# Metaformer block on one core: router chain rewritten, convolution entered before all queries are made, band products inside the norm

## The chip, the cores and the metric

One core of one Trainium2 chip runs the whole kernel. The metric is device microseconds (us) of one execution, median of the runs. Engines are called by the profile's names: PE is the matrix engine (PEld its weight loads), DVE the vector engine, ACT the scalar engine, POOL the GpSimd engine, SP the engine whose queue issues most DMA transfers (a DMA moves data between HBM and SBUF, or inside SBUF). SBUF is the working memory with 128 partitions, PSUM the eight banks that PE writes. Each engine works through its own instructions in order and waits on semaphores.

## The reference, cut to what matters

```python
# x: (8, 128, 16, 16), that is 2048 tokens (8 images x 256 places) of 128 channels
n   = layernorm(x)                          # over channels, here in chunks of 512 tokens
qkv = conv1x1(n, w_qkv)                     # 384 channels: queries, keys, values of 8 heads
agg = conv1x1_grouped(conv5x5_depthwise(qkv, w_dw), w_pw)
for h in (qkv heads, agg heads):            # linear attention, relu on q and k
    out = q @ (k^T [v, 1]),  divided by its last column
x = x + batchnorm(conv1x1(out, w_proj))
# mixture of experts 0: 8 experts, width 512, gelu, best 2 of 8 by t @ gate_w.T
# then softmax attention over the 256 places of an image (adds to x)
# mixture of experts 1: 16 experts, width 256, silu(gate) * up, best 2 of 16
```

Both mixtures see tokens normalised over channels; the kernel normalises them with a centred product and a per-token scale.

## The kernel before, in words

**Opening.** `layer_norm` on PE makes, for each of four chunks c of 512 columns, the centred chunk (L1131), then 4 products for the variance (L1138), then the product that spreads the inverse root over the partitions (`ln_spread`, L1148). DVE (`ln_scale`) makes the diagonal for it (L787) and multiplies (L794), giving `xn`. `turn_weights` transposes the weights of queries, keys and values and the small convolution weights inside the norm (L1161 to L1166). `keep_clock` (L1120) are products whose result nobody uses. `head(n, c)` (L1175) is the 1x1 convolution of chunk c; n counts keys, values, queries. ACT evicts each (L579; for queries also through a relu into `q_relu`, L578).

**Bands.** Eight band products (L1187) and one spread (L1192) lay the depthwise and pointwise weights out over the partitions; ACT evicts all nine (L586, L590, semaphore `band_out`). From `dw_band` and `pw_in`, POOL and DVE multiply the weights of the convolution, `cw` (`build_weights`, L321): for each of 12 units four groups, two by POOL and two by DVE, three units ahead of PE at most. A unit is 32 channel groups of keys, values or queries: units 0 to 3 are keys, 4 to 7 values, 8 to 11 queries.

**Convolution.** 48 steps s, four a unit, each ten PE instructions (L1281) on `cmap`, the maps that SP fetches from `heads_raw` unit by unit (L391). PE enters the loop only when all 12 head evictions, the late weight transposes (L1201) and the router product (L1257) are done. `STEPS` says at which s the stages of the first linear attention (L1212 turn, L1224, L1237, L1249) come between: for image n at s = 3n + 1. The second attention, on the convolution's output, comes from s = 38 on.

**Router r (0 and 1).** `token_norm` on PE makes, for 16 tiles of 128 tokens, the centred rows and the logits (L1315) in six banks. ACT evicts the logits (L667), squares the rows (L655), takes roots (L660). DVE then runs a chain in which each `step` waits for the one ahead: the best expert, a mask, the second best (L918 to L924), `chosen` (L926, written with its axes turned), and after PE's counts (`slots`: L1326 to L1338) the slot of each token (L936 to L946), the one-hot tables `block_hot`, `block_val`, `place_hot` (L951 to L956), with which PE inverts the table (L1345). DVE reads the result as `token` and `dest` (L976 to L978). The inverse root `tok_inv` (L900) is made in two halves, one ahead of the slots, one between the two `place_hot`. ACT scales the rows with it (L683, `token_rows`), SP stores them (L363), and POOL gathers the rows of each block by `token` (L518) for the experts (L1379 transposes them, L1369 and L1390 are the two expert products).

POOL also makes tables once, in the opening: `place_id` (128 x 4096), `passed`, and others (L487).

Of the kernel before, what the change touches and what calls it, by code (L numbers as in the profile page):

```python
# [32 lines left out]
F16 = mybir.dt.float16  # L33
# [27 lines left out]
STEPS = {3 * n + 1: (0, n) for n in range(B + 3)} | {4 * 2 * UPT + 6 + n: (1, n) for n in range(B + 1)}  # L61
# [37 lines left out]
def metaformer(nc, x, w_qkv, w_dw, w_pw, w_proj, bn_gamma, bn_beta, bn_mean, bn_var,  # L99
# [10 lines left out]
    with ctx:  # L110
# [15 lines left out]
        place_id = sb("place_id", [128, 128, 2 * TT], F16)  # L126
        pair_id = sb("pair_id", [128, 2, TT], F16)
# [36 lines left out]
        hots = sb("hots", [128, 2, TT, E1])  # L164
# [7 lines left out]
        slot_f = sb("slot_f", [128, 2, TT])  # L172
        slot_i = sb("slot_i", [128, 3, 2, TT], I32)
# [82 lines left out]
        band_mm, band_out = sem("band_mm"), sem("band_out")  # L256
# [180 lines left out]
        def _(pool):  # L437
# [51 lines left out]
            table(place_id[:, :, :], [[1, 128], [0, 2 * TT]], 0, 0)  # L489
# [4 lines left out]
            table(passed[:, :, :], [[128, NI1], [-128, E1 - 1]], 0, 0)  # L494
# [3 lines left out]
            pool.affine_select(out=passed[:, :, :], in_=passed[:, :, :], compare_op=ALU.is_ge, fill=1e6,  # L498
                               base=NB - 1, pattern=[[-1, NI1], [1, E1 - 1]], channel_multiplier=0).then_inc(tables, 1)
# [3 lines left out]
            pool.wait_ge(band_out, 9)  # L503
            for u in range(len(UNITS)):
                for i in (0, 2):
                    build_weights(pool, u, i)

            def moe_pool(r, E):
# [5 lines left out]
                pool.wait_ge(rt_table, 4 * r + 3)  # L514
# [7 lines left out]
                pool.wait_ge(rt_table, 4 * r + 4)  # L522
# [12 lines left out]
        def _(act):  # L535
# [33 lines left out]
            def heads(n, t):  # L569

                for c in range(NCH):
                    act.wait_ge(qkv_mm, NCH * n + c + 1)
                    src = bank[c][:, :].rearrange("p (b y x) -> p b y x", b=2, y=HW)

                    def to(m):
                        return m[:, :, :, 2 * c:2 * c + 2].rearrange("p x y b -> p b y x")
                    if t == 0:
                        act.activation(to(q_relu), src, ACT.Relu).then_inc(q_relued, 1)  # L578
                    act.activation(to(heads_raw[t]), src, ACT.Copy).then_inc(head_a, 1)  # L579

            heads(0, ORDER[0])

            for k in range(9):
                act.wait_ge(band_mm, k + 1)
                if k < 8:
                    act.activation(dw_band[:, :, :, 2 * k:2 * k + 2].rearrange("p k g x -> p x (k g)"),  # L586
                                   bank[4 + k % 4][:, 0:2 * KS * NG].rearrange("p (x n) -> p x n", x=2),
                                   ACT.Copy).then_inc(band_out, 1)
                else:
                    act.activation(pw_in[:, :, :].rearrange("p o g -> p (o g)"), bank[4][:, 0:G8 * NG],  # L590
                                   ACT.Copy).then_inc(band_out, 1)
            for n in (1, 2):
                heads(n, ORDER[n])

            act.wait_ge(w_ready, 6)
            act.activation(bn[:, 0:1], vec("var"), ACT.Sqrt, bias=eps[:, 2:3]).then_inc(bn_step, 1)
# [21 lines left out]
            for s in range(GU * len(UNITS)):  # L618
                if s in STEPS:
# [28 lines left out]
            def token_scales(r):  # L648
# [14 lines left out]
                for g, tiles in enumerate(ROW_GROUPS):  # L663
                    act.wait_ge(rows_mm, 6 * r + g + 1)
                    a, n = tiles[0], len(tiles)
                    src = bank[ROW_BANKS[r][g]][:, 0:n * (C + E)].rearrange("p (t q) -> p t q", t=n)
                    act.activation(tok_lg[:, a:a + n, 0:E], src[:, :, C:C + E], ACT.Copy).then_inc(tok_logits, 1)  # L667
                    if g < 4:
                        squares(tiles)
                    if g == 3:  # L670
                        roots(0)
                squares(range(12, TT))
# [6 lines left out]
            def token_rows(r):  # L679
                for i in range(TT):  # L680
                    if i % 8 == 0:
                        act.wait_ge(tok_scale, 2 * r + i // 8 + 1)
# [3 lines left out]
            def moe_act(r, E, NI):  # L686
                m = moe[r]
                if r == 0:
                    act.wait_ge(moe_w[0], 48)
                    act.wait_ge(rt_table, 1)  # L690
# [80 lines left out]
        def _(dve):  # L771
# [26 lines left out]
            def conv_weights():  # L798
# [4 lines left out]
                dve.wait_ge(dw_zero, 1)  # L803
                dve.tensor_copy(dw_t[0:G8 * KS, :, :].rearrange("p k g -> p (k g)"), bank[1][0:G8 * KS, 0:KS * NG])\
                    .then_inc(w_ready, 1)
                dve.tensor_copy(pw_t[:, :, :].rearrange("p o g -> p (o g)"), bank[2][0:G8, 0:G8 * NG])\
                    .then_inc(w_ready, 1)

            ln_scale(0, conv_weights)
            dve.wait_ge(w_turned, 2)  # L810
            dve.tensor_copy(wT[:, W_P0:W_P0 + 4, :], bank[6][:, :].rearrange("p (j q) -> p j q", q=128))\
                .then_inc(w_ready, 1)
# [692 lines left out]
```

## Time and profile before

| | us |
|---|---|
| median of 3 runs (lowest, highest) | 446.61 (446.04, 447.75) |
| the profiled execution | 449.81 |
| its span, first to last instruction | 448.1 |
| PE busy, share of the span | 374.2 (84%) |
| DVE, ACT, POOL busy | 238.8, 191.2, 192.3 |
| PE's share of the chain that ended last | 66% |
| mean granted clock of PE | 0.895 |

PE busy is the time with a matmul in flight; the chain is the sequence of work, followed back from the last instruction, in which each piece released the next. Only what lies on it sets the time. The granted clock is a share of 2.4 GHz; its two levels are 1.00 (2.4 GHz) and 0.50 (1.2 GHz), and a stretch between them contains a change.

### The profile page before, as it was taken

How to read it: one execution, taken by the hardware profiler on the slowest of the kernel's cores; microseconds unless marked ns; L12 is line 12 of the kernel's file. 1: busy time of each engine (PE TensorE's matmuls, PEld its weight loads, DVE VectorE, ACT ScalarE, POOL GpSimd, SP SyncE). 2: the span in 40 equal slices, each digit the busy share in tenths (PEclk: the TensorE clock that was granted, in tenths of full speed). 3: DMA queues.
4: the chain of work that ended last, by engine and by line, in shares of the span. 5: the costliest groups of instructions: out<-in, count | busy, mean ns of one | idle time of the engine just before them, and what ended most of it. 6: DMA issues, size and time to landing. Idle time of an engine off the chain costs nothing.

```text
span 448.1 us, 7846 instructions
## 1 busy us (share of the span) xinstructions
PE 374.2 (84%) x2499; PEld 318.3 (71%) x2499; DVE 238.8 (53%) x589; ACT 191.2 (43%) x512; POOL 192.3 (43%) x206
## 2 busy tenths in 40 slices
PE   6998799999989837999999569989636999999903
PEld 3673799999969524999999536665423998888802
DVE  2611355455126382566777457476584466567515
ACT  3089223322322644677666256385443233222213
POOL 9916055356000306777775500000306777566620
PEclk9599699999998965899999969999956799999965
DMA  5013045455238522895111160000012112111146
GB/s 153 0 24 78 17 67 85 62 88 78 28 47 278 145 69 61 266 309 150 55 55 41 38 189 0 1 0 0 1 57 69 54 52 54 42 42 43 42 118 187
DMA packets 44015, 35.27 MB, mean 79 GB/s; under 512 B 3800, under 2 KB 39752, under 8 KB 43976
## 3 DMA queue, kind: packets, MB, share of 16 engines
q1 hardware_dynamic: 36412, 24.70, 21.6%
q0 software_dynamic: 4096, 8.40, 6.4%
q10 hardware_dynamic: 3468, 1.67, 2.6%
q8 instruction: 22, 0.36, 0.4%
q14 instruction: 17, 0.14, 0.1%
HBM read 21.12 MB, written 7.34 MB: 64 GB/s over the span
## 4 chain that ended last, share of the span: by engine, by line
PE 66%; DVE 9%; ACT 7%; DMA 7%; issue 4%; POOL 3%; SPq 1%; ACTq 1%; DVEq 1%; POOLq 0%
PE bank L1369 16%; PE bank L1281 11%; PE bank L1390 10%; PE bank L1237 3%; POOL x_rows L518 3%; PE bank L1131 2%; DMA x_rows<-tok,token 2%; PE bank L1148 2%; DMA ln_sq<-y 2%; ACT heads L579 2%; PE bank L1138 2%; PE bank L1416 2%; PE bank L1457 2%; PE bank L1224 2%; PE bank L1120 2%
## 5 line engine op out<-in xcount | busy, mean ns | idle before, releaser
L1369 PE MATMUL bank<-x_cols,w_block 128*128 x688 | 99.6, 291 | 7.9 <-DVE w_block L1019 5.0
L1369 PEld LDWEIGHTS bank<-x_cols,w_block 128*128 128x128 f32 x688 | 88.7, 202 | 13.5 <-issue 12.3
L518 POOL DMA_INDIRECT x_rows<-tok,token x64 | 61.7, 964 | 52.5 <-DMA tok<-ln_sq 33.6
L525 POOL DMA_INDIRECT y<-wide,dest x64 | 63.2, 987 | 34.2 <-DVE wide L1054 25.6
L1390 PE MATMUL bank<-w_down,h_cols 128*128 x500 | 71.7, 281 | 1.7 <-DVE wide L1054 1.7
L1390 PEld LDWEIGHTS bank<-w_down,h_cols 128*128 128x128 f32 x500 | 64.2, 196 | 2.2 <-issue 2.0
L1281 PE MATMUL bank<-cmap,cw 128*128 128x112 f32 (+2 forms) x480 | 59.0, 281 | 0.3 <-DVE tok_w L854 0.3
L321 POOL TENSOR_TENSOR cw<-pw_in,dw_band 128x640 f32<-128x640 f32 x24 | 37.2, 1571 | 49.6 <-PE bank L1281 38.6
L1281 PEld LDWEIGHTS bank<-cmap,cw 128*128 128x128 f32 x480 | 57.5, 198 | 0.5 <-DVE tok_w L854 0.5
L512 POOL MEMSET wide<- 128x4096 f32 x2 | 7.0, 3511 | 100.5 <-DVE xs L1105 60.6
L1034 DVE TENSOR_TENSOR h_cols<-h_in,bank 128x256 f32<-128x256 f32 x47 | 19.7, 419 | 30.2 <-PE bank L1390 15.1
L1026 DVE TENSOR_TENSOR h_in<-bank,wT 128x512 f32<-128x512 f32 x39 | 27.0, 691 | 16.4 <-PE bank L1369 13.9
L710 ACT ACTIVATE h_cols<-h_in 128x512 f32<-128x512 f32 x39 | 24.6, 630 | 24.1 <-PE bank L1390 19.9
L702 ACT ACTIVATE x_cols<-bank 128x128 f32<-128x128 f32 x64 | 15.4, 270 | 37.9 <-PE bank L1379 37.9
L716 ACT ACTIVATE h_in<-bank 128x256 f32<-128x256 f32 x47 | 18.0, 383 | 30.9 <-PE bank L1369 30.9
L321 DVE TENSOR_TENSOR cw<-pw_in,dw_band 128x640 f32<-128x640 f32 x24 | 23.0, 991 | 5.7 <-PE bank L1281 5.7
L1120 PE MATMUL bank<-ones,ident 128*128 128x512 f32 x24 | 18.2, 893 | 7.3 <-DMA ln_sq<-y 7.3
L699 ACT ACTIVATE w_block<-w_up 128x512 f32 x39 | 23.9, 614 | 0.2 <-PE bank L1369 0.2
L824 DVE TENSOR_TENSOR kvm<-bank,blk 128x128 f32<-128x128 f32 x16 | 4.7, 291 | 34.9 <-PE bank L1224 34.9
L1019 DVE COPY w_block<-w_up 128x512 f32 x47 | 20.9, 447 | 3.1 <-issue 2.4
L725 ACT ACTIVATE wide<-wide,pair_w 128x128 f32<-128x128 f32 x32 | 10.2, 389 | 24.5 <-DMA ln_sq<-y 24.5
L1379 PE MATMUL bank<-ident,x_rows 128*128 128x128 f32 x64 | 15.8, 298 | 4.2 <-DMA x_rows<-tok,token 4.2
(209 smaller groups left out, 602.3 us busy)
## 6 DMA issues: line engine op xcount, KB each, us to landing
cmap<-heads SPq DMA_DIRECT2D x48, 64.0 KB
w_up<-in_L_ffn_w_dram SPq DMA_DIRECT2D x1, 2048.0 KB, 8.7
tok<-ln_sq SPq DMA_DIRECT2D x8, 256.0 KB, 2.3
w_up<-in_L_ffn_gate_w_dram SPq DMA_DIRECT2D x4, 512.0 KB
w_up<-in_L_ffn_up_w_dram SPq DMA_DIRECT2D x4, 512.0 KB
w_down<-in_L_ffn_down_w_dram SPq DMA_DIRECT2D x4, 512.0 KB
wide<-y SPq DMA_DIRECT2D x8, 256.0 KB, 4.5
ln_sq<-y SPq DMA_DIRECT2D x8, 256.0 KB, 5.0
```

The lines of the kernel that those rows point to most:

```text
L321: engine.tensor_tensor(cw[:, u % CWR, i, :, :].rearrange("p k (o x) -> p k o x", x=HW), pw_in[:, :, g].unsqueeze(1).unsqueeze(3).broadcast ...
L518: pool.indirect_dma_start(out=x_rows[:, j % RING, :], out_offset=None, in_=tok_dram[r], in_offset=bass.IndirectOffsetOnAxis(ap=token[r][:, ...
L525: pool.indirect_dma_start(out=y_dram[r], in_=y_acc[:, s * C:(s + 1) * C], in_offset=None, out_offset=bass.IndirectOffsetOnAxis(ap=dest[r][ ...
L699: act.activation(w_block[:, n % 3, :], w_up0[:, bass.ds(e * F0, F0)], ACT.Copy).then_inc(m.w, 1)
L710: act.activation(h_cols[:, j % 2, :], h_in[:, j % 2, :], ACT.Gelu_apprx_tanh)\
L1019: dve.tensor_copy(w_block[:, j % 3, :], w_up[:, bass.ds(e[j] * UP, UP)]).then_inc(m.w, 1)
L1026: dve.tensor_tensor(h_in[:, j % 2, :].rearrange("p (k s) -> p k s", k=M0), bank[2 + j % 2][:, :].rearrange("p (k s) -> p k s", k=M0), wT[: ...
L1034: dve.tensor_tensor(h_cols[:, j % 2, 0:F1], h_in[:, j % 2, 0:F1], bank[2 + j % 2][:, F1:2 * F1], ALU.mult).then_inc(m.h_in, 1)
L1120: pe.matmul(bank[b][:, :], ident[:, :], ones[:, :].unsqueeze(1).broadcast_to([128, 4, 128]), start=True, stop=True)
L1281: mm = pe.matmul(bank[b][:, i * 128 + y0 * B:i * 128 + y1 * B], cw[:, u % CWR, i, k, :], cmap[:, t, v * GU + i, (y0 + k - EDGE) * B:(y1 + ...
L1369: mm = pe.matmul(bank[2 + j % 2][:, i * 128:(i + 1) * 128], w_block[:, j % 3, i * 128:(i + 1) * 128], x_cols[:, bass.ds(at[j], 128)], star ...
L1390: mm = pe.matmul(bank[6 + j % 2][:, 0:C], h_cols[:, j % 2, i * 128:(i + 1) * 128], w_down[:, bass.ds(ej * (K * C) + i * C, C)], start=(i = ...
```

## The change

In the opening, all four variance groups now come first on PE, then `turn_weights`; the unused product of `keep_clock` is gone; spreads, band products and the heads of keys are woven together. ACT evicts bands 0 to 3 and the spread, DVE bands 4 to 7; ACT instead of DVE evicts `dw_t` and `pw_t`. `q_relu` is made by one DVE instruction from `heads_raw`. PE enters the convolution after 10 of the 12 heads; the last two come at s = 2 and 3, the late transposes at s = 6, the router product at s = 10. The first attention starts at s = 12, one image every two and a half steps. POOL makes `place_id`, a new table `block_id`, and `passed` between the `cw` builds. In the router, DVE evicts the logits, `chosen` is written in the order of memory, the slots take four steps, `tok_inv` is one instruction directly behind `chosen`, and `token` and `dest` come ahead of the item tables; POOL waits for `token` alone.

```diff
-STEPS = {3 * n + 1: (0, n) for n in range(B + 3)} | ...
+STEPS = {12 + 5 * n // 2: (0, n) for n in range(B + 3)} | ...
+        BAND_BANKS = (3, 4, 5, 4, 6, 7, 5, 4)
+        PW_BANK = 6
+        HEAD_BANKS = ((0, 1, 2, 3), (7, 5, 4, 6), (2, 3, 7, 5))
 # PE, opening
-            layer_norm(0, lambda c: (x_in[c], 16), between=turn_weights, after=lambda c: head(0, c))
-            (eight band products, the spread, heads 1 and 2, late transposes)
+            for c in range(NCH):
+                pe.wait_ge(x_in[c], 16)
+                pe.matmul(bank[c][:, :], center[:, :], chunk(xs, c), start=True, stop=True).then_inc(ln_cent, 1)
+            (four variance groups)
+            turn_weights()
+            spread_scale(0)
+            spread_scale(1)
+            band_product(0)
+            head(0, 0)
+            spread_scale(2)
+            band_product(1)
+            head(0, 1)
+            spread_scale(3)
+            band_product(2)
+            head(0, 2)
+            band_product(3)
+            head(0, 3)
+            for k in range(4, 8):
+                band_product(k)
+            (the spread of pw_t)
+            for c in range(NCH):
+                head(1, c)
+            head(2, 0)
+            head(2, 1)
 # PE, in the loop of 48 steps
+                if s in (2, 3):
+                    head(2, s)
+                if s == 6:
+                    turn_late()
+                if s == 10:
+                    (router product)
+                if s == 12:
+                    pe.wait_ge(q_relued, 1)
+                    pe.wait_ge(router_out, 1)
 # ACT
+            for k in range(4):
+                act.wait_ge(band_mm, k + 1)
+                act.activation(dw_band[...], bank[BAND_BANKS[k]][...], ACT.Copy).then_inc(band_act, 1)
+                head_copy(0, k)
 # DVE, in the loop of 48 steps
+                if s == 4:
+                    dve.wait_ge(head_a, 3 * NCH)
+                    dve.tensor_scalar(q_relu[...], heads_raw[0][...], 0.0, None, ALU.max).then_inc(q_relued, 1)
+                if s == 7:
+                    late_weights()
 # POOL
             for u in range(len(UNITS)):
                 for i in (0, 2):
                     build_weights(pool, u, i)
+                if u == CWR - 1:
+                    table(place_id[:, :, :], [[1, 128], [0, 2 * TT]], 0, 0)
+                if u == CWR:
+                    table(block_id[:, :, :], [[128, NB], [0, 2 * TT]], 0, 0)
+                if u == CWR + 1:
+                    table(passed[:, :, :], [[128, NI1], [-128, E1 - 1]], 0, 0)
 # DVE, router
-        hots = sb("hots", [128, 2, TT, E1])
+        hots = sb("hots", [128, 2, E1, TT])
+                dve.tensor_tensor(chosen[:, 0:E, :], hots[:, 0, 0:E, :], hots[:, 1, 0:E, :], ALU.add).then_inc(rt_mask, 1)
+                token_inverse(r)
+                step(dve.tensor_tensor(both, both, slot.unsqueeze(1).broadcast_to([128, 2, E, TT]), ALU.mult))
+                step(dve.tensor_reduce(slot_i[...], both.rearrange("p k e t -> p k t e"), AX.X, ALU.max))
+                step(dve.tensor_tensor(slot_parts[...], slot_i[...], low_high[:, :, :], ALU.bitwise_and))
+                step(dve.tensor_copy(place[...], slot_parts[:, :, :]))
 # PE, end of slots
-                keep_clock(1, 2)
+                pe.wait_ge(rows_copied, TT * (r + 1))
+                keep_clock(4, 2)
```

## Rows read from the trace of the kernel before

**Rows 1.** The chain of waits, opening: start us, us, what, count.
```profile
10.00 2.67 PE bank L1138 x24
...
14.56 2.00 PE bank L1120 x2
16.57 1.71 PE bank L1148 x2
18.27 1.50 PE bank L1138 x8
...
23.91 0.86 PE bank L1175 x2
...
27.53 6.48 PE bank L1187 x32
...
46.08 0.91 ACT heads L579
...
48.00 2.47 PE bank L1281 x10
```

**Rows 2.** Busy time by stretch: stretch, length, busy PE, PEld, DVE, ACT, POOL, clock, DMA.
```profile
18.00:22.00 4.00, 4.00 (x12) 2.72 (x11) 2.98 (x7) 0.26 (x1) 4.00 (x6) 0.50 0.00 0
22.00:24.00 2.00, 2.00 (x5) 0.89 (x4) 1.24 (x4) 0.91 (x1) 1.85 (x4) 0.85 0.01 4
...
52.00:54.00 2.00, 2.00 (x14) 2.00 (x14) 0.00 (x0) 0.02 (x1) 0.00 (x0) 0.67 0.00 0
```

**Rows 3.** Timeline of PE: start us, us, engine, line, operation, count, [idle before].
```profile
41.75 0.82 PE L1201 MATMUL bank<-ident,wraw 128*128 128x128 f32 x6
...
101.60 7.97 PE L1281 MATMUL bank<-cmap,cw 128*128 128x128 f32 x70
110.35 0.46 PE L1212 MATMUL bank<-ident,wide 128*128 128x128 f32 x2 [0.79 <-DMA heads<-conv_out]
```

**Rows 4.** Timeline of SP's queue while the first maps are fetched.
```profile
28.67 16.46 SPq L391 DMA_DIRECT2D cmap<-heads  x20
```

**Rows 5.** Timeline of POOL: the largest table, and builds of `cw`.
```profile
15.93 4.18 POOL L487 IOTA place_id<- 128x4096 f16 x1
...
35.53 7.81 POOL L321 TENSOR_TENSOR cw<-pw_in,dw_band 128x640 f32<-128x640 f32 x6 [11.03 <-ACT pw_in L590]
...
107.42 3.86 POOL L321 TENSOR_TENSOR cw<-pw_in,dw_band 128x640 f32<-128x640 f32 x2 [0.62 <-PE bank L1281]
```

**Rows 6.** Timeline around router 0.
```profile
150.19 3.87 PE L1315 MATMUL bank<-tok_w,xs 128*128 128x136 f32 x32
...
154.97 0.29 DVE L918 TENSOR_REDUCE rv<-tok_lg 128x16 f32<-128x128 f32 x1 [3.83 <-ACT tok_lg L667]
...
158.53 0.69 DVE L926 TENSOR_TENSOR chosen<-hots 128x128 f16<-128x128 f32 x1
...
160.36 0.17 DVE L936 COPY ends<-bank 128x8 f32<-128x8 f32 x1 [0.28 <-PE bank L1338]
...
162.41 0.69 DVE L951 TENSOR_TENSOR block_hot<-place_id,place 128x1024 f16<-128x1024 f16 x1
...
167.80 0.18 DVE L977 TENSOR_SCALAR token<-place_of 128x32 int32<-128x32 int32 x1
...
169.92 1.14 POOL L518 DMA_INDIRECT x_rows<-tok,token  x1 [15.21 <-DMA tok<-ln_sq]
```

**Rows 7.** Timeline around router 1.
```profile
320.43 0.42 DVE L918 TENSOR_REDUCE rv<-tok_lg 128x16 f32<-128x256 f32 x1 [3.98 <-ACT tok_lg L667]
...
325.45 1.23 DVE L926 TENSOR_TENSOR chosen<-hots 128x256 f16<-128x256 f32 x1
...
333.60 2.45 PE L1345 MATMUL bank<-block_val,place_hot 128*128 128x32 f16 x32 [5.33 <-DVE place_hot L956]
...
336.92 0.17 DVE L976 CAST place_of<-bank 128x32 int32<-128x32 f32 x1
...
338.38 1.23 POOL L518 DMA_INDIRECT x_rows<-tok,token  x1 [18.36 <-DMA tok<-ln_sq]
```

More of the change, by code:

```diff
@@ L488, in table @@
                           allow_small_or_imprecise_dtypes=True).then_inc(tables, 1)
-            table(place_id[:, :, :], [[1, 128], [0, 2 * TT]], 0, 0)
+            table(low_high[:, 0, :], [[0, 2 * TT]], 127, 0)
+            table(low_high[:, 1, :], [[0, 2 * TT]], (NB - 1) * 128, 0)
             table(pair_id[:, 0, :], [[128, TT]], 0, 1)
@@ L581, in _ @@
[L581 to L596, printed above, removed]
+            act.wait_ge(w_turned, 1)
+            act.wait_ge(dw_zero, 1)
+            act.activation(dw_t[0:G8 * KS, :, :].rearrange("p k g -> p (k g)"), bank[1][0:G8 * KS, 0:KS * NG], ACT.Copy)\
+                .then_inc(dw_ready, 1)
+            act.activation(pw_t[:, :, :].rearrange("p o g -> p (o g)"), bank[2][0:G8, 0:G8 * NG], ACT.Copy)\
+                .then_inc(dw_ready, 1)
@@ L598, in kv_copy @@
+            act.wait_ge(band_mm, 9)
+            act.activation(pw_in[:, :, :].rearrange("p o g -> p (o g)"), bank[PW_BANK][:, 0:G8 * NG],
+                           ACT.Copy).then_inc(band_act, 1)
+            for n in (1, 2):
+                for c in range(NCH):
+                    head_copy(n, c)
             def kv_copy(h, b):
@@ L917, in router @@
-                for src, top, oh in ((lg, m1, oh1), (l2, m2, oh2)):
-                    step(dve.tensor_reduce(top, src, AX.X, ALU.max))
-                    step(dve.tensor_tensor(eq, src, per_e(top), ALU.is_equal))
-                    step(dve.tensor_tensor(sc, eq, rk, ALU.mult))
+                    dve.wait_ge(tables, 15 + E1)
+                step(dve.tensor_reduce(m1, lg, AX.X, ALU.max))
+                step(dve.tensor_tensor(eq, lg, per_e(m1), ALU.subtract))
+                for oh in (oh1, oh2):
+                    if oh is oh2:
+                        step(dve.scalar_tensor_tensor(out=l2, in0=oh1, scalar=MASKED, in1=eq,
+                                                      op0=ALU.mult, op1=ALU.add))
+                        step(dve.tensor_reduce(d, l2, AX.X, ALU.max))
+                        step(dve.tensor_tensor(l2, l2, per_e(d), ALU.subtract))
+                    step(dve.scalar_tensor_tensor(out=sc, in0=(eq if oh is oh1 else l2), scalar=0.0, in1=rk,
+                                                  op0=ALU.is_ge, op1=ALU.mult))
@@ L921, in router @@
                     step(dve.tensor_reduce(mx, sc, AX.X, ALU.max))
                     step(dve.tensor_tensor(oh, sc, per_e(mx), ALU.is_equal))
-                    if oh is oh1:
-                        step(dve.scalar_tensor_tensor(out=l2, in0=oh1, scalar=MASKED, in1=lg,
-                                                      op0=ALU.mult, op1=ALU.add))
-                dve.tensor_tensor(chosen[:, 0:E, :].rearrange("p e t -> p t e"), oh1, oh2, ALU.add).then_inc(rt_mask, 1)
-                step(dve.tensor_tensor(d, m2, m1, ALU.subtract))
+                dve.tensor_tensor(chosen[:, 0:E, :], hots[:, 0, 0:E, :], hots[:, 1, 0:E, :], ALU.add).then_inc(rt_mask, 1)
@@ new lines, in _ @@
+            turn_weights()
[11 more added lines that the diff above has]
+            head(0, 3)
+            for k in range(4, 8):
+                band_product(k)
+            pe.wait_ge(band_dve, 1)
+            pe.wait_ge(dw_ready, 2)
+            pe.matmul(bank[PW_BANK][:, 0:G8 * NG], spread[:, :, :].rearrange("p i x -> p (i x)"),
+                      pw_t[:, :, :].rearrange("p o g -> p (o g)"), start=True, stop=True).then_inc(band_mm, 1)
```

208 lines of the change are left out of this document (113 added, 95 removed).

## Prediction

> **What bounds the kernel now.** I read the page first: the chain that ended last is mostly PE, so I asked of each stage whether PE, or something that PE waits for, ends last. The chain of waits over the opening gives the answer for that part [rows 1]: PE carries it to the band products, and then it changes to ACT, whose evictions of the heads follow each other at 0.91 us until 46.99. PE has nothing to do in that time; the convolution starts only at 48.00. The busy time by stretch shows what the pause costs besides [rows 2]: the clock is 0.50 when the convolution starts and reaches 1.00 only at 53.3 (a mean of 0.67 over 52 to 54 is 0.68 us at the full level). The same view shows 0.50 from the norm to 22.6. In the convolution itself the timeline of PE shows ten instructions in 1.11 us (7.97 over 7 steps plus a little overhead) without gaps, but for one of 0.79 [rows 3]: that stage is PE's alone. The timelines of the two routers show the reverse [rows 6, 7]: PE waits, DVE's chain of small steps sets the time, and at its end POOL's first gather waits not for the token table (ready at 167.98) but for the stored rows, until 169.92.
>
> **The opening, after.** I take PE's order and add the durations. The variances of three chunks end at 12.67 as before. The fourth, 1.50 at the lower level, to 14.2; the transposes take 1.9 (12.67 to 14.56 before), to 16.1; two spreads at 1.71, to 19.5 [rows 1]. DVE has both diagonals by 14.7, ahead of PE. What follows on PE up to the convolution, at the full level: eight band products at 0.81 (6.48 / 8), ten heads and two spreads at 0.86, the last spread of weights some 0.86: 6.5 + 10.3 + 0.9 = 17.7, so 37.2. At the lower level PE takes double. Before, dense work from 14.56 had the clock up at 22.6, with sparse variances (1.50, one column each) in between [rows 1, 2]. After, dense work starts at 16.1 and is not interrupted, so I put the rise between 19.5 and 22.6: 0 to 1.5 us lost, 0.7 taken. Start of the convolution: 37.9 instead of 48.00, 10.1 earlier.
>
> What could be late instead: ACT alternates a band (0.81) and a head (0.91) while PE needs 2.5 for such a pair and a spread, so it keeps up; it has the last band and `pw_in` by 33.5. DVE evicts bands 4 to 7, which the trace has only on ACT. From 480 columns in order to twice that, 0.65 to 1.2 each, four of them end by 32.7 or 34.3; `cw` is then begun at 33.5 to 34.4 and the first group is there at 36.4 at the latest. The maps: the fourth key eviction is at 29.8 instead of 28.6, four issues at 0.82 [rows 4] end at 33.1, plus some 2 to land: 35.1. All are ahead of 37.9, by 1.5 at the least. Only head products, then, stand between; the words "while values and queries are still made" are true of two heads on PE and of eight evictions on ACT.
>
> **The convolution, after.** PE's work in it grows by two heads (1.7), the late transposes (0.82 and one more, 1.0) [rows 3] and the router product (0.3): 3.0. It no longer begins at 0.50: 5.3 us at half speed cost 2.65 [rows 2]. The gap of 0.79 goes, because it waits for aggregated values sent just ahead of s = 38, and the steps of the first attention now lie in front (s up to 37) and give the transfers 3.8 us more. Net: 10.1 - 3.0 + 2.65 + 0.8 = 10.5 us.
>
> Moved past other queues: POOL's builds now have the tables between them. Six builds took 7.81 alone, and two took 3.86 beside DVE's [rows 5], so from 33.5 six end at 41.3 to 45.1, `place_id` (4.18) at 45.5 to 49.3, and unit 3 is built at 48.1 to 53.2. PE wants it at 37.9 + 12 x 1.11 + 3.0 = 54.2. The next tables are smaller and each unit then takes twice as long on PE, so it is covered by 1 to 6 us. Behind DVE's relu at s = 4, which waits for the twelfth eviction (about 44), are builds for unit 3 (wanted at 54) and the late weights (wanted at s = 10, some 51.6): covered by 2 us or more. SP has for a unit 3.3 of maps and 1.4 of sends against 4.45 on PE, but starts four units ahead.
>
> The Trainium skill (SBUF — State Buffer, "Who interferes with whom") says that a DVE instruction with two SBUF inputs, or in a two-port mode, and a GpSimd instruction take a shared port for the whole instruction, so that one of them blocks. The rows agree as far as they go, 1.30 for a POOL build alone and 1.93 beside DVE. By the rule the relu (an estimate of 1.3 us) could wait for all of `place_id`; by the rows 4.18 at most, which still leaves the wanted time of the late weights about met.
>
> **Router 0.** Logits: the last rows are made at 154.06; DVE evicts them itself (0.2) as the groups come and starts its first step near 154.5 instead of 154.97: 0.5. The number of steps to the masks is 11 before and 11 after: 0. `chosen` in order of memory: 0.69 becomes 0.29, the length of the steps of that size: 0.4. From the counts to `block_hot` 2.05 us are spent (160.36 to 162.41); after, a product and a reduction of 256 columns (0.42 each, as in router 1), a mask and a cast (0.2 each) with 0.03 between: 1.34, so 0.7. No reciprocal between the two `place_hot`: 0.1. End: the rows are scaled right after `chosen` (158.6), 16 at 0.27 and 2.3 for the last store, so at 165.3, and the gather waits for `token` instead (about 166.3): 169.92 - 167.98 = 1.95 more. Sum 3.65 [rows 6].
>
> Against it: both masks are now written with a stride. Below, nothing. Above, as `chosen` was: (1.23 - 0.42) / 256 = 3.2 ns more an element [rows 7], 0.8 us here and 1.6 in router 1. The nearest row for 4-byte elements is ACT's strided eviction of a head, 0.91 / 512 = 1.8 ns against 1.0 ns on DVE ((0.42 - 0.29) / 128): 0.8 more, so 0.2 and 0.4; I take those. And PE's two unused products (some 3.4 at the lower level) now end at about 169.3, where the first gathered rows land, and ACT's table loads end near the same time: 0.35 lost. Router 0: 3.1 us.
>
> **Router 1.** The same with 256 columns: logits 0.6, `chosen` 1.23 to 0.42 0.8, slots 0.7, reciprocal 0.1. PE's inversion ends at 336.05 but DVE reads it at 336.92, behind the item tables; that order is turned: 0.9. `token` is ready at 337.3 and the gather starts at 338.38, waiting for stored rows: 1.1. Less 0.4 for the stride, and 0.1 for PE's unused products: 3.7 us [rows 7].
>
> **Sum.** 10.5 + 3.1 + 3.7 = 17.3. Of the profiled execution, 449.81, that leaves 432.5 (span 430.8); the median of the runs is 3.2 lower than that execution, so I forecast 446.6 - 17.3 = 429.3.
>
> **Rivals.** (a) As summed, 425.5 to 432: 0.62. Its low end is the strides at nothing (0.6), the clock up at once (0.7), and a shorter low stretch at the start of the experts, where PE begins closer behind its unused products (2); its high end the other bounds.
> (b) Strides cost what `chosen` did: 0.6 more in router 0, 1.2 more in router 1, and 1 for the evictions of bands if those then pass the heads: 432. For it, only the 2-byte row; against it, ACT's. Chance 0.12. The Trainium skill (SBUF — State Buffer, "Door 1: The DMA port swizzle") says that each access which crosses into a new 16-byte line pays a penalty, which would make this stride dear; the rows show it for ACT's and for `chosen`.
> (c) The builds set the pace: POOL at 1.93 a build and blocked by DVE besides; if every table costs as much as `place_id`, units 3 to 5 each come 1.5 to 2 late and 5 us of the 10.5 go: 434.3. For it, two builds of 3.86; against it, the slack above. Chance 0.12.
> (d) Gathers don't start earlier, because the stored rows still land last: 3.05 of the routers goes, 432.4. Against it, 165.3 against 166.3. Chance 0.07.
> (e) Slower: the clock isn't granted with bands, heads and waits for evictions alternating. At 0.50 to the end of the heads and 5.3 us into the convolution, PE gets to it at 19.5 + 35.4 = 54.9, 6.9 later; with the 3.0 added, 0.8 saved, and 6.8 from the routers that is 2.3 us slower, 448.9. It decides only if the low stretch goes on past about 50; before, the clock came up under the same products with longer pauses. Chance 0.02.
> (f) The change does not do what it says: ACT's evictions or maps still hold the start back, say by 6 us, to 435.5. Chance 0.05.
>
> **How the numbers follow.** (a) to (d) lie within 424.5 and 435; (e), most of (f) and the tail of (c) and low tail of (a) are left out. A measurement of this kernel tells 0.5% (2.2 us) from no change; only (e) and some joint mishap come that near: faster 0.96, same 0.02, slower 0.02.
>
> **What would show it.** In the profile after: the first L1281 instruction (its new line) near 38 at clock 1.00, PE without a gap of over 0.5 from 16 to the end of the convolution, which ends at 119.8 instead of 130.4; no idle time of PE put down to `cw`; `chosen` at 0.29 and 0.42 us; the first gather released by `token`, 12 us after the last row product instead of 15.9 (router 0). It is wrong if PE waits for `cw` in units 3 to 5, if the clock is 0.50 after 24, or if a gather still waits for the store.

## The result: 14.1 us faster, where 17.3 were forecast

| | before | after |
|---|---|---|
| median of the runs on one chip (lowest, highest), us | 447.18 (446.04, 453.52), 4 runs | 433.13 (431.46, 440.12), 4 runs |
| ratio after / before, 95% interval | | 0.9685 (0.9639 to 0.9731) |
| the same as time, 447.18 x (1 - ratio) | | -14.1 (-12.0 to -16.1) |
| convolution starts, us (one profile each) | 48.00 | 37.27 |
| convolution ends | 130.38 | 119.23 |
| router 0: last row product to the first expert product | 19.68 | 16.99 |
| router 1: the same | 22.65 | 19.89 |

The forecast was 429.3, with a range of 424.5 to 435.0. The execution that was profiled is the slowest of its four (440.12, span 438.0; the others have spans of 429.4 to 432.1), so below stages are compared, not totals. Its extra time sits in two stages behind router 0: from the first expert product to the second norm it took 94.4 us (90.7 in the profile before), and in the second norm 28.3 (25.1).

**The opening, after.** The chain of waits, opening (start us, us, what); it answers to [rows 1]:

```profile
3.71 6.26 PE bank L1233 x8
9.97 4.35 PE bank L1237 x32
16.22 3.39 PE bank L1214 x4
...
28.01 3.24 PE bank L1226 x16
32.08 5.35 PE bank L1208 x12
37.43 2.22 PE bank L1355 x20
...
117.01 2.22 PE bank L1355 x20
119.23 2.59 PE bank L1365 x6
```

There is no ACT in it: centring (L1233), variances (L1237), spreads (L1214), bands (L1226), heads (L1208) and the convolution (L1355) are all PE's. The pause of [rows 1] is gone. The busy time by stretch shows where the clock still falls; it answers to [rows 2]:

```profile
10.00:12.00 2.00, 2.00 (x20) 2.00 (x20) 1.80 (x4) 1.31 (x4) 1.93 (x2) 1.00 0.31 87
12.00:14.00 2.00, 2.00 (x13) 2.00 (x14) 1.97 (x3) 0.26 (x1) 1.93 (x3) 0.59 0.00 0
14.00:16.00 2.00, 2.00 (x18) 1.66 (x18) 0.68 (x1) 0.26 (x1) 1.86 (x22) 0.50 0.00 0
16.00:18.00 2.00, 2.00 (x5) 0.84 (x3) 0.00 (x0) 0.73 (x2) 1.02 (x9) 0.50 0.00 0
18.00:20.00 2.00, 2.00 (x6) 1.20 (x5) 1.70 (x4) 0.00 (x0) 0.00 (x0) 0.71 0.00 0
36.00:38.00 2.00, 2.00 (x11) 1.28 (x10) 2.00 (x2) 2.00 (x4) 2.00 (x2) 1.00 0.41 77
```

0.50 from 12.3 to 19.2, behind the one-column products of the variances, and 1.00 where the convolution starts. PE's waits in the convolution and POOL's timeline there (answering to [rows 3, 5]):

```profile
PE bank L1292 <- ACT kvT L622: 1.1, 2, 0.6
```
```profile
36.51 7.54 POOL L324 TENSOR_TENSOR cw<-pw_in,dw_band 128x640 f32<-128x640 f32 x4
44.01 5.20 POOL L494 IOTA place_id<- 128x4096 f16 x1
49.19 3.26 POOL L324 TENSOR_TENSOR cw<-pw_in,dw_band 128x640 f32<-128x640 f32 x2
52.41 1.16 POOL L494 IOTA block_id<- 128x1024 f16 x1
53.54 3.22 POOL L324 TENSOR_TENSOR cw<-pw_in,dw_band 128x640 f32<-128x640 f32 x2
```

PE never waits for `cw`, though unit 3 is built only at 52.45 and PE comes to it (s = 12) at 54.07. Nor does it wait for values sent by DMA.

**The router, after** (answering to [rows 6]; the timeline of router 0):

```profile
143.37 0.29 DVE L945 TENSOR_REDUCE rv<-tok_lg 128x16 f32<-128x128 f32 x1
...
144.66 0.37 DVE L956 TENSOR_TENSOR hots<-rt,rv 128x128 f32<-128x128 f32 x1
...
147.18 0.29 DVE L957 TENSOR_TENSOR chosen<-hots 128x128 f16<-128x128 f32 x1
...
148.42 0.42 DVE L970 TENSOR_TENSOR hots<-hots,bank 128x256 f32<-128x256 f32 x1 [0.33 <-PE bank L1412]
...
148.87 0.58 DVE L971 TENSOR_REDUCE slot_i<-hots 128x32 int32<-128x256 f32 x1
...
149.98 0.69 DVE L980 TENSOR_TENSOR block_hot<-block_id,place 128x1024 f16<-128x1024 f16 x1
...
155.42 0.18 DVE L993 TENSOR_SCALAR token<-place_of 128x32 int32<-128x32 int32 x1
...
156.49 1.15 POOL L534 DMA_INDIRECT x_rows<-tok,token  x1 [12.70 <-DVE dest L994]
```

`chosen` takes 0.29, as forecast. The gather is released by DVE and no longer by the stored rows (four stores are issued from 148.83 to 152.28 and land 2.4 later, by 154.7). But `token` is written at 155.60 and the gather begins at 156.49: 0.88 us in which nothing in the profile runs for it. Router 1 has the same, 328.36 to 329.14. The prediction's sign was a gather 12 us behind the last row product of router 0; it is 13.4 (15.9 before).

### The profile page after: what moved, and what is told of

Read it like the earlier page. It is cut to its first block, busy times and chain, and to the rows that moved or that the text cites. A ratio compares the mean times of both kernels' runs of the same rounds, so it can differ in the third digit from the quotient of the medians.

```text
span 438.0 us, 7838 instructions
## 1 busy us (share of the span) xinstructions
PE 369.9 (84%) x2497; PEld 314.8 (72%) x2497; DVE 250.4 (57%) x594; ACT 184.7 (42%) x494; POOL 196.3 (45%) x209
## 2 busy tenths in 40 slices
DMA packets 44014, 35.26 MB, mean 80 GB/s; under 512 B 3800, under 2 KB 39752, under 8 KB 43976
## 4 chain that ended last, share of the span: by engine, by line
PE 71%; DVE 10%; DMA 7%; issue 4%; POOL 3%; ACT 2%; SPq 1%; ACTq 1%; DVEq 1%; POOLq 0%
PE bank L1444 16%; PE bank L1355 12%; PE bank L1465 10%; PE bank L1305 4%; DMA x_rows<-tok,token 3%; POOL x_rows L534 2%; PE bank L1208 2%; DMA ln_sq<-y 2%; PE bank L1491 2%; PE bank L1389 2%; PE bank L1292 2%; PE bank L1532 2%; PE bank L1226 1%; PE bank L1233 1%; PE bank L1454 1%
## 5 line engine op out<-in xcount | busy, mean ns | idle before, releaser
L1444 PE MATMUL bank<-x_cols,w_block 128*128 x688 | 98.4, 288 | 7.8 <-DVE w_block L1045 4.7
L1444 PEld LDWEIGHTS bank<-x_cols,w_block 128*128 128x128 f32 x688 | 87.6, 200 | 13.1 <-issue 12.1
L1355 PE MATMUL bank<-cmap,cw 128*128 128x112 f32 (+2 forms) x480 | 57.5, 275 | 0.0
L1355 PEld LDWEIGHTS bank<-cmap,cw 128*128 128x128 f32 x480 | 55.8, 192 | 1.5 <-issue 1.4
L324 POOL TENSOR_TENSOR cw<-pw_in,dw_band 128x640 f32<-128x640 f32 x24 | 39.9, 1684 | 34.5 <-PE bank L1355 18.9
L324 DVE TENSOR_TENSOR cw<-pw_in,dw_band 128x640 f32<-128x640 f32 x24 | 27.7, 1179 | 3.8 <-PE bank L1355 3.4
L1146 PE MATMUL bank<-ones,ident 128*128 128x512 f32 x22 | 16.2, 871 | 7.8 <-DMA ln_sq<-y 7.8
L1454 PE MATMUL bank<-ident,x_rows 128*128 128x128 f32 x64 | 15.7, 292 | 6.3 <-DMA x_rows<-tok,token 6.3
L1075 DVE TENSOR_TENSOR y_part<-bank,b_all 128x128 f32<-128x128 f32 x39 | 11.4, 291 | 16.1 <-PE bank L1465 15.6
```

What stands on the lines that cost most here:

```text
L324: engine.tensor_tensor(cw[:, u % CWR, i, :, :].rearrange("p k (o x) -> p k o x", x=HW), pw_in[:, :, g].unsqueeze(1).unsqueeze(3).broadcast ...
L1355: mm = pe.matmul(bank[b][:, i * 128 + y0 * B:i * 128 + y1 * B], cw[:, u % CWR, i, k, :], cmap[:, t, v * GU + i, (y0 + k - EDGE) * B:(y1 + ...
L1444: mm = pe.matmul(bank[2 + j % 2][:, i * 128:(i + 1) * 128], w_block[:, j % 3, i * 128:(i + 1) * 128], x_cols[:, bass.ds(at[j], 128)], star ...
L1454: pe.transpose(bank[k % 2][:, 0:128], x_rows[:, k % RING, :], ident[:, :]).then_inc(m.turned, 1)
```

## The experiments

Twelve runs in three sets, each set on another chip. On those chips the stage of experts 0 takes some 100 us instead of 80 in every kernel, the kernel before too (482 to 484 us in all), so ratios and stages are compared, and only within a set where fractions count.

### The change split in two

`before_again` and `after_again` are the two kernels. `open_only` has the opening and the convolution of after and the routers of before; `router_only` the reverse:

```diff
 open_only (from after)
-        hots = sb("hots", [128, 2, E1, TT])
+        hots = sb("hots", [128, 2, TT, E1])
-                pool.wait_ge(rt_table, 4 * r + 1)
+                pool.wait_ge(rt_table, 4 * r + 3)
 (and the rest of the router as before)
```

> The kernel before, for a second profile. Theory A (parts of the 449.81 us of the first profile were chance: its clock was 0.50 in stretches where other executions have 1.00): another profile has a span nearer to 445, and the stages differ from the first by up to 3 us where the clock changes level. Theory B (the change lost some of what its trace shows gained): the stages repeat within 0.5 us and the span is 448 again.

> The kernel after, again. Both theories: 431 to 434 us. In a profile that is not disturbed I expect the convolution to start at 37.4 and the norm ahead of the softmax attention to take 25 us, as before (28 in the first profile after, where the clock fell to 0.50 from 265 to 271).

> The change's opening and convolution, with the routers of before. By my sum -10.5 us; by the first profiles -11.2 (convolution's end at 119.2 against 130.4). If a rival holds by which the saved time comes back later: -8 or less.

> The change's routers, with the opening of before. By my sum -6.8 us (3.1 and 3.7); by the first profiles -5.2 (2.5 and 2.8: last row product to first expert product). Theory A: this and the opening alone add up to the whole within 1.5 us. Theory B: they add up to more than the whole by 3.

| | ratio (95%) | convolution starts, ends | router 0, 1: last row product to first expert product |
|---|---|---|---|
| `before_again` | (484.39 us, one run) | 43.23, 125.46 | 19.52, 22.58 |
| `after_again` | 0.9767 (0.9726 to 0.9807) | 37.67, 119.51 | 17.26, 19.81 |
| `open_only` | 0.9812 (0.9763 to 0.9861) | 38.00, 120.61 | 19.51, 22.78 |
| `router_only` | 0.9883 (0.9842 to 0.9924) | 48.12, 130.43 | 17.03, 19.91 |

What follows: each part does its own work. Of 484 us the opening gives 9.1 (6.7 to 11.5) and the routers 5.7 (3.7 to 7.6); together 14.8, where the whole change gives 11.3 (9.3 to 13.3) on that chip. The parts add up to 3.5 more than the whole. That misses the 1.5 of theory A and is what theory B said, but the three intervals together leave some 3.7 us of room, so the totals decide nothing. The stages do add up: `after_again` ends the convolution within 1.1 us of `open_only` (119.51, 120.61), and its routers are within 0.3 us of those of `router_only` (17.26 and 19.81 against 17.03 and 19.91). No interaction shows in them.

The surprise is the row of `before_again`: 43.23, not 48.00. Its busy time by stretch (first fence) and its chain (second), against [rows 1, 2]:

```profile
12.00:14.00 2.00, 2.00 (x19) 1.20 (x20) 1.97 (x3) 0.26 (x1) 1.93 (x3) 1.00 0.00 0
14.00:16.00 2.00, 2.00 (x12) 1.51 (x12) 1.58 (x3) 0.11 (x1) 1.86 (x22) 1.00 0.00 0
...
42.00:44.00 2.00, 1.39 (x5) 1.27 (x6) 1.93 (x7) 0.27 (x2) 0.00 (x0) 0.54 0.06 15
44.00:46.00 2.00, 2.00 (x12) 2.00 (x11) 0.18 (x1) 0.00 (x0) 0.00 (x0) 0.50 0.00 0
```
```profile
13.15 1.06 PE bank L1120 x2
14.21 0.87 PE bank L1148 x2
...
31.16 3.82 ACT heads L579 x4
...
43.23 2.47 PE bank L1281 x10
```

It is the same kernel, but here the clock did not fall in the norm, and everything behind it comes 4.8 us earlier. The fall of [rows 2] happens in some executions only. That is theory A, with more than the 3 us that it allowed a stage. The base row of my sum was one with the fall.

### The low clock at the start of the convolution

`pause_filled` is the kernel before with six unused products in PE's pause:

```diff
+            keep_clock(4, 6)
             pe.wait_ge(head_a, 3 * NCH)
```

> The kernel before, with six products whose result nobody uses put into PE's pause ahead of the convolution (5.2 us of work into a pause of 5.5). If the low clock at the convolution's start comes from the pause: clock 1.00 through it, and the convolution (first to last instruction) takes 79.7 us instead of 82.4. If the clock falls there for another reason, it stays at 82.4. In time: 2 to 2.6 us less than before. Its opening also is a further sample of how the clock goes in the norm of before: start of the convolution near 48 with the clock at 0.50 from 12 on, or near 43 without.

Measured: ratio 0.9997 (0.9945 to 1.0049). The stretches of its profile, to be held against those of `before_again`:

```profile
42.00:44.00 2.00, 1.66 (x7) 0.84 (x6) 1.34 (x7) 0.33 (x2) 0.00 (x0) 1.00 0.04 9
44.00:46.00 2.00, 2.00 (x20) 2.00 (x19) 0.74 (x2) 0.35 (x2) 0.00 (x0) 1.00 0.00 0
```

1.00 throughout, and the convolution takes 79.27 us instead of 82.23 to 82.38: 2.96 to 3.1 (forecast 2.65). As the unused products run on a little, the loop begins 0.57 later, and its end, 123.07 against 125.46, is 2.4 earlier. The whole time, forecast 2 to 2.6 us shorter, came out 0.1 shorter and doesn't show that; its interval, -2.7 to +2.4 us, just holds it, so the stage is shown and the sum is not.

### Entering the convolution before the last heads

`late_start` is the kernel after with the two last heads, the late transposes and the router product put back ahead of the loop:

```diff
+            head(2, 2)
+            head(2, 3)
+            turn_late()
+            (router product)
-                if s in (2, 3):
-                    head(2, s)
-                if s == 6:
-                    turn_late()
```

> The kernel after, but PE enters the convolution only after all twelve heads, the late transposes and the router product. By my theory (most of the opening's gain is band products and heads without a pause, and one clock change less) the convolution starts 4.0 us later (two heads, transposes, product: 3.0, and 1 of waiting) and takes 3.0 less, so the whole loses 1 to 1.5 us. If entering early is what gives the gain: 5 us or more are lost, and the clock falls again ahead of the convolution.

Measured: ratio 0.973 (0.9619 to 0.9841), convolution from 39.59 to 118.70, 79.11 long. The plain order in the same set (`layout_back`, whose opening is that of after) runs from 34.75 to 116.94, 82.19 long. Of the 4.8 us by which the loop begins earlier, 3.1 are work that was only moved into it, and 1.8 us are left. Of these, 0.5 are not the edit's: in `late_start` the variances already begin 0.55 later (9.37 against 8.82), and the low stretch in the norm is 3.4 us long in both. Entering early gives 1.2 us, inside the 1 to 1.5 that was expected; in `late_start` PE waits 1.3 us for the late weights (`wT`, DVE) just ahead of the loop. The whole times (0.973 and 0.9703) don't tell the two apart.

### The layout of the masks

`layout_back` is after with the masks as before, so that `chosen` is written turned and everything else in order:

```diff
-        hots = sb("hots", [128, 2, E1, TT])
+        hots = sb("hots", [128, 2, TT, E1])
-                dve.tensor_tensor(chosen[:, 0:E, :], hots[:, 0, 0:E, :], hots[:, 1, 0:E, :], ALU.add)
+                dve.tensor_tensor(chosen[:, 0:E, :].rearrange("p e t -> p t e"), oh1, oh2, ALU.add)
```

> The kernel after, with the masks in the layout of before (and so chosen written with its axes turned). By the first profile after, the new layout costs 0.08 at each of three steps and 0.16 at the reduction in router 0 and gives 0.40 at chosen; in router 1, 0.17 at three and 0.33, against 0.80. So this kernel takes the same time, within 0.2 us from last row product to inversion. If the new layout were worth what I forecast for it (0.2 + 0.4): 0.6 us slower.

Measured: ratio 0.9703 (0.9618 to 0.9787); from the last row product to the end of the inversion 11.94 and 15.00 us, as in after (11.94 to 11.98, 14.96 to 15.00). Its timeline against that of after:

```profile
142.28 0.29 DVE L956 TENSOR_TENSOR hots<-rt,rv 128x128 f32<-128x128 f32 x1
142.61 0.29 DVE L949 SCALAR_TENSOR_TENSOR rt<-hots,rt 128x128 f32<-128x128 f32 x1
...
144.55 0.69 DVE L957 TENSOR_TENSOR chosen<-hots 128x128 f16<-128x128 f32 x1
...
146.64 0.42 DVE L971 TENSOR_REDUCE slot_i<-hots 128x32 int32<-128x256 f32 x1
```

The turned `chosen` costs 0.40 more, the strided masks 2 x 0.08 for writing, 0.08 for reading them back and 0.16 in the reduction: 0.40. The layout is worth nothing in either router. A stride costs per instruction what its rows show; it was only moved.

### Why the gather starts late

`items_first` is after with the first two item instructions (`beyond`, `item`) moved ahead of DVE's wait for the inversion:

```diff
+                (beyond and its reduction)
                 dve.wait_ge(rt_inverse, r + 1)
                 (place_of, token, dest)
-                (beyond and its reduction)
```

> The kernel after, with the mask and sum of the item tables ahead of DVE's wait for the inversion, so that only short instructions follow token. Theory A, POOL needs 0.8 to 0.9 us from token to its first gather whatever DVE does: the same distance, router 0 unchanged, router 1 some 0.4 us later (1.8 us of work in a wait of 1.4). Theory B, DVE's long instructions behind token hold POOL back: the distance shrinks to 0.3, and router 0 gains 0.5.

Measured: ratio 0.9697 (0.9592 to 0.9802). The delay behind `token` stayed 0.88 and 0.78 us; in router 1 the edit costs besides (inversion to gather 1.78 instead of 1.29, because DVE reads the inversion later). So DVE's following instructions are not the cause.

The later scatters give the next thought: in the same trace they begin 0.28 us behind the DVE instruction that they wait for, and there POOL has worked a microsecond earlier. Ahead of the first gather it has had nothing for 12.7 us. `warm_awake` gives it a one-column memset in router 0 alone; it also puts one unused product ahead of PE's first centring:

```diff
+                if r in (0,):
+                    pool.wait_ge(rt_inverse, r + 1)
+                    pool.memset(stir[:, r:r + 1], 0.0)
                 pool.wait_ge(rt_table, 4 * r + 1)
...
+            keep_clock(7, 1)
             for c in range(NCH):
                 pe.wait_ge(x_in[c], 16)
```

> The changed kernel with two edits in different places. (1) One unused 512-column product on PE ahead of the first centred chunk. In the changed kernel PE idles until 3.7 us, and the weight loads of the centring then follow each other at 0.86 us, twice the 0.43 of later 512-column passes, until about 8.3: the first products run at the lower rate. Theory W (the rate rises a certain time after PE starts to be busy): the unused product, from about 2.2 to 3.9, brings the rise from 8.3 to about 6.7, the variances start about 0.7 earlier (9.1 instead of 9.8), the convolution starts 0.6 earlier. Rival: the chunks are paced by the arrival of x, and nothing moves or all comes 0.2 later. (2) In router 0 alone POOL does a one-column memset when the inversion is done (rt_inverse), just ahead of its wait for the token table. In every run of the changed routers the first gather began 0.88 (router 0) and 0.78 us (router 1) after the token table was written, while scatters later in the stage begin 0.28 after the DVE instruction that they wait for. Theory Q (POOL, after 12 us without work, takes 0.6 us longer to start): with the memset the first gather of router 0 begins 0.3 after token, that of router 1, without it, still 0.78. Rival R (it is in the gather itself, which reads a table that was written just before): 0.88 stays in router 0. Whole time 0 to 1.2 us less than the changed kernel.

Measured: ratio 0.9718 (0.9666 to 0.977). Router 0, with the memset, and router 1, without it:

```profile
154.48 0.10 POOL L533 MEMSET stir<- 128x1 f32 x1 [11.41 <-PE bank L1424]
154.69 0.18 DVE L997 TENSOR_SCALAR token<-place_of 128x32 int32<-128x32 int32 x1
155.27 1.15 POOL L538 DMA_INDIRECT x_rows<-tok,token  x1 [0.69 <-DVE dest L998]
...
342.50 0.18 DVE L997 TENSOR_SCALAR token<-place_of 128x32 int32<-128x32 int32 x1
343.46 0.99 POOL L538 DMA_INDIRECT x_rows<-tok,token  x1 [15.94 <-DVE dest L998]
```

154.87 to 155.27 is 0.40 instead of 0.88; 342.68 to 343.46 is still 0.78. `joined`, below, has the memset in both routers and 0.40 and 0.29. So the start comes 0.48 earlier, where theory Q said 0.6. But an earlier start is not an earlier end. In router 0 the gather takes 1.15 us with and without the memset. In router 1 it took 0.99, and in `joined` it takes 1.45:

```profile
343.21 0.89 DVE L1003 TENSOR_TENSOR beyond<-ends,passed 128x705 f32<-128x705 f32 x1
343.51 1.45 POOL L538 DMA_INDIRECT x_rows<-tok,token  x1 [0.59 <-DVE dest L998]
```

It ends 1.75 us behind `token`, against 1.77 without the memset, so nothing is won there. DVE's `beyond` runs over the first 0.59 us of this gather; in router 0 it takes 0.44 and is over within 0.04 of the gather's start. Whether `beyond` holds the gather is not shown; no run separates it. Accordingly the first expert product comes 0.2 to 0.5 us earlier in router 0 and no earlier in router 1 (19.81; 19.68 to 20.05 without the memset).

Nor is the idle time of theory Q shown to be the cause. Two scatters in `after_third`, each released by DVE (222.38 and 424.83):

```profile
222.66 0.97 POOL L541 DMA_INDIRECT y<-wide,dest  x1 [3.33 <-DVE wide L1080]
...
425.64 0.98 POOL L541 DMA_INDIRECT y<-wide,dest  x1 [1.33 <-DVE wide L1080]
```

After 3.33 us without work the first begins 0.28 behind its release, after 1.33 us the second 0.81. The second is the 18th scatter of router 1, and it is late by 0.81 in all fourteen profiles, before and after, with 1.3 to 2.4 us of idle time; others begin at 0.28 after up to 3.6 us. That delay goes with a place in POOL's program. The memset both ends the idle time and puts another instruction ahead of the gather, so its 0.48 doesn't tell the two apart, and the cause stays open. Rival R in its plain form, a cost in the gather itself, would have left 0.88 in router 0 and is refuted there.

The unused product ahead of the centring did nothing: the first variance product starts at 9.02 (9.01 in `joined`), against 8.95 in `after_third`, because PE waits for x by DMA between the chunks. Theory W is neither shown nor refuted: the distance of 0.86 between products ends at 5.8 in `warm_awake`, but at 7.3 in `joined` with the same edit, and at 7.0 to 10.1 without it.

### Holding the clock in the norms

`norm_held` is after with an unused product ahead of the third variance of each norm; `joined` is that and both edits of `warm_awake`, with the memset in both routers; `after_third` is after itself, for this set.

```diff
                 pe.wait_ge(ln_sqd, c + 1)
+                if c == 2:
+                    keep_clock(7, 1)
                 (four variance products)
```

> The changed kernel with one more unused 512-column product (0.86 us at the full level) ahead of the variance of the third chunk, in the norm of the opening and in the second norm. The clock fell to 0.50 during the one-column products of the variances in most executions of the changed kernel (from 12.4 to 19 in the opening), and in the second norm in about half (28.3 instead of 25.1 us from the turn to the scores). Theory H (the fall follows from the sparse one-column products): with the unused product the clock stays at 1.00 in both norms; the convolution starts at 33.8 + 0.9 = 34.7 instead of 37.3 to 38.0, the second norm takes 25.1 + 0.9 = 26.0; against the changed kernel's mean some 2 us less in the opening and 0.7 less in the second norm, whole time 1 to 3 us less. Rival (the clock's fall does not depend on this): the clock falls as often, and each norm costs 0.9 to 1.7 more, whole time 2 us more.

> All the edits of the two other runs together, with the memset on POOL in both routers. If W, Q and H hold: convolution starts at 34.1, first gathers 0.3 us after token in both routers, second norm 26.0; whole time 3 to 4 us under the changed kernel of the same call, ratio to the kernel before about 0.962. If none holds: 2 us over the changed kernel.

> The changed kernel itself, as the one to compare with in this call. Ratio to the kernel before 0.969 to 0.977 as in the calls before; the first gathers 0.88 and 0.78 us after token; the convolution starts at 37.3 to 38.0 if the clock falls in the norm, near 34 if it does not.

| | median us | ratio (95%) | clock in the first norm | convolution starts | second norm, turn to scores |
|---|---|---|---|---|---|
| `after_third` | 469.34 | 0.9726 (0.9656 to 0.9796) | 0.50 from 14.0 to 17.4 | 35.26 | 28.29 |
| `warm_awake` | 466.33 | 0.9718 (0.9666 to 0.9770) | 0.50 from 12.3 to 19.1 | 36.50 | 28.53 |
| `norm_held` | 465.77 | 0.9689 (0.9628 to 0.9751) | 1.00 | 34.24 | 26.12 |
| `joined` | 468.05 | 0.9723 (0.9673 to 0.9772) | 0.50 from 13.9 to 20.7 | 37.42 | 27.64 |

Both runs with the unused product, by stretch; the first fence is of `norm_held`, the second of `joined`:

```profile
12.00:14.00 2.00, 2.00 (x19) 1.83 (x19) 1.97 (x2) 0.53 (x2) 1.93 (x3) 1.00 0.00 0
14.00:16.00 2.00, 2.00 (x18) 1.19 (x17) 0.92 (x2) 0.73 (x2) 1.86 (x22) 1.00 0.00 0
```
```profile
14.00:16.00 2.00, 2.00 (x15) 1.32 (x14) 0.68 (x1) 0.73 (x2) 1.86 (x22) 0.50 0.00 0
...
20.00:22.00 2.00, 2.00 (x5) 0.97 (x5) 0.45 (x1) 1.50 (x2) 0.00 (x0) 0.82 0.00 0
```

In `norm_held` the clock stays up in both norms, and both stages take the length that was forecast (34.24 against 34.7, 26.12 against 26.0). In `joined`, with the same product at the same place, it falls in both norms all the same (27.64 in the second). So one unused product doesn't hold the clock, and theory H in the form that I gave it fails; `items_first` held it without one. None of the four ratios is told from another. The kernels that could be better than after (0.9689 and 0.9718 against 0.9726) are within their intervals: no version was shown to beat it.

## Why the prediction was right, and where its sizes were off

**The opening.** PE's order and durations carried it. In the profile after, the convolution was forecast for 37.9 and starts at 37.27, its end for 119.8 and 119.23; extra work 3.0 against 82.0 - 79.1 = 2.9; no gap for DMA, no wait for `cw`; 1.00 where the loop begins. The maps, the evictions on DVE and the late weights had the cover they were given. Two choices in it stand differently now. The value of the clock at the start was 3.0, not 2.65. And the base row was one of two kinds of execution. Without the fall the start moves from 43.23 to 33.83 (`items_first`), 9.4 us. With it, it moves from 48.00 and 48.12 (low for 10.2 us) to 37.27 to 38.00 where the clock was low for 6.8 us, and to 34.75 and 35.26 where it was for 3.4: 10.0 to 13.4. The forecast of 10.1 lies in this, but the one pair of profiles that it was held against could have given 5 to 14. The end of the convolution, as a mean over profiles with the plain opening of each kind, falls from 128.8 (three) to 118.4 (six): 10.4, against 10.5 forecast. So near a hit is partly luck: one in three and one in six of these profiles are without the fall.

**The routers: the step that was mis-sized is that the gather starts when `token` is there.** Up to the inversion the terms hold: 13.47 to 11.96 in router 0 (1.5 forecast: 0.5 + 0.4 + 0.7 + 0.1 - 0.2) and 16.47 to 14.96 in router 1 (1.5 against 1.8). Within that, the stride was set at 0.2 and 0.4 and cost 0.40 and 0.82 with its reads (in router 1 0.59 for each of two writes, and 0.58 for one read, that take 0.42 in order, and 1.01 for a reduction that takes 0.69). The interval from the inversion to the gather went from 2.39 to 1.39 and from 2.33 to 1.29, 1.0 each, where 1.95 and 0.9 + 1.1 were forecast. The missing 0.88 and 0.78 are what POOL needs from `token` to the gather, a term that the sum put at nothing; even the quick scatters need 0.28. A memset ahead of it took 0.48 of each away, which brought the first expert product forward in router 0 and not in router 1; what the 0.48 comes from is open. In router 0 PE's unused products cost nothing against the 0.35 I had taken off. In router 1 the first gather itself got shorter, 1.23 to 0.99, which no term had. As means over the profiles of each kind the routers are 2.5 and 2.7 shorter instead of 3.1 and 3.7, 1.6 us less.

**The rest of the difference,** 17.3 - 1.6 = 15.7 against 14.1 (12.0 to 16.1), is inside the interval. One thing could fill it and is open: the second norm took 25.05, 28.38, 25.55 and 25.09 us in the four profiles of kernels with the opening of before, and 28.25, 25.23, 25.26, 27.36, 28.38, 27.06, 28.29 and 28.53 in eight with that of after (over 27 where the clock falls there). The mean is 1.3 us longer, but four against eight draws of the same chance can do that.

**The rivals.** (b) Strides as dear as `chosen`: no, a 4-byte stride cost 0.08 us for 128 elements and 0.17 for 256, the 2-byte one 0.40 and 0.80. The Trainium skill (SBUF — State Buffer, "Door 1: The DMA port swizzle") has a penalty for each access that crosses into a new 16-byte line; by that alone both strides would pay one for each element, and the rows differ fivefold. (c) Builds on POOL: they came within 1.6 us of mattering (52.45 against 54.07), with `place_id` at 5.20 instead of 4.18. (d) Stored rows last: no, they land by 154.7, the table at 155.6. (e) The clock: no, 1.00 from 19.2. (f) Evictions or maps: no, neither is in the chain of the opening.

The shared port shows in the norm, in the diagonal that DVE makes at 11.45 while POOL's select on `band` runs from 10.48 to 13.36:

```profile
11.45 2.42 DVE L799 TENSOR_TENSOR ln_diag<-ident,ln_r 128x512 f32<-128x512 f32 x1
...
13.98 0.69 DVE L799 TENSOR_TENSOR ln_diag<-ident,ln_r 128x512 f32<-128x512 f32 x1
```

It ends at 13.87, 0.51 behind POOL's select, though it needs 0.69 by itself. With the rule of the Trainium skill (SBUF — State Buffer, "Who interferes with whom"), that of a two-input DVE instruction and a GpSimd one that reads SBUF one waits for the other, this agrees to 0.18 us. In thirteen of the fourteen profiles this product begins behind the select, at 10.51 to 12.16, and ends at 13.86 to 13.88; in `layout_back` it begins at 10.46, just ahead of it, takes 0.69, and the select takes 3.41 instead of 2.88. It costs nothing in the profile after, where PE comes to the spread at 16.2, but where PE is early it does: 0.31 us in `after_third`.

The same happened to the relu, for which the prediction named a wait of 4.18 at most. Where it begins first (43.65 in after), it takes 1.49, and `place_id`, 0.36 behind it, takes 5.20. In `late_start` the order is turned:

```profile
41.46 4.19 POOL L494 IOTA place_id<- 128x4096 f16 x1
42.11 4.62 DVE L870 TENSOR_SCALAR q_relu<-heads 128x2048 f32<-128x2048 f32 x1
```

The relu takes 4.62 us and ends 1.08 behind `place_id`. PE wants it only at s = 12, so nothing was lost.

## What to carry over

Check with a second profile whether the row that a sum starts from repeats: the clock of a sparse stretch made 4.8 us of difference in one and the same kernel. When a wait is removed, the waiting engine doesn't start when the table is ready: its own start has to stand in the sum as a term, here 0.3 to 0.9 us, and one row doesn't price it (the same gather began 0.29 behind a landed store and 0.88 behind DVE). Judge an edit by the end of an instruction and not by its start: 0.48 us of earlier start were worth nothing in router 1. And a layout that makes one instruction cheap has to be priced over every reader and writer: here 0.40 was taken from one and given to four.

## What the runs showed of the hardware that I had not expected

- POOL's first gather began 0.88 and 0.78 us behind its release by DVE after 12.7 and 15.8 us without work, and 0.40 and 0.29 with a one-column memset just ahead. Idle time alone doesn't make the delay: released by landed stores after 15.2 us, with the table long there, it had begun 0.29 behind the landing [rows 6], and the 18th scatter of router 1 is late by 0.81 after 1.3 to 2.4 us, in every profile. What makes it is open.
- The clock in a norm is a draw: in the opening it fell in ten of the fourteen profiles of this case, for 3.4, 6.8 or 10.2 us, and it fell and did not fall in one and the same kernel (`before` and `before_again`).
- In the first microseconds the rows give 1.00 as the granted clock, but the 512-column products follow each other at 0.86 us, and at 0.43 only from 5.8 to 10.1 on. The trace has no record of the clock ahead of that point: its first one begins at 5.5 in `warm_awake`, 8.9 in after and 10.1 in `open_only`, where the distance changes, and the 1.00 of the rows ahead of it stands for no record. With that point the start of the variances varies, from 8.8 to 10.5.
